# First piece of w1 on ScalarE's DMA queue, two chunk pairs of the weights loaded ahead of x, and the head's products and conversions reordered

## The chip, the cores and the metric

The kernel runs on one core of a Trainium2 chip. The metric is device time in microseconds (us); a run's time is a little longer than its span, which goes from the first to the last instruction of the profiled execution. A measurement of this kernel can tell some 0.2% (0.56 us) from no change.

## The reference, cut to what matters

```python
# x: (4, 512, 512), all in float32; w1, w2: (512, 512)
attn = einsum('ds,td->st', w1, w2) * sparse_mask            # "the mask product"
x = x + gelu(einsum('bds,st->bdt', layernorm(x), attn) + b2) # stage 1
x = x + clustered_ffn(layernorm(x))                          # stage 2
x = x + attention(layernorm(x))                              # stage 3
x = x + clustered_ffn(layernorm(x))                          # stage 4
```

Only the part that has to come before everything else, here called the head, is touched: loading w1 and w2, their product, and the normalized first batch of x that stage 1 multiplies with that product.

## The kernel before, in words

Every engine works through a list written out by hand (`PE_ORDER`, `ACT_ORDER`, `DVE_ORDER`, `POOL_ORDER`, `SP_ORDER`), strictly in order; a step whose input isn't ready holds up all behind it. A step is named kind.key. The steps of the head:

- `load.*` (SyncE, SP): DMA issues. w1 and w2 come in four row chunks each (`load.w1.c`, `load.w2.c`), the first batch of x in four token tiles (`load.x0.t`), the mask in four chunks (`load.sparse.c`), the stage 2 weight in four (`load.ffn.c`); each is 256 KB. `load.cen` is 128 KB.
- Each float32 operand is split in a high and a low part, so that a product is three matmuls (hi*hi, lo*hi, hi*lo). `w1hi.c` (line L558) and `w2hi.c` (L554) on ScalarE (ACT) round a chunk, `w1lo.c` (L743) and `w2lo.c` (L738) on VectorE (DVE) take the remainder.
- `attn.0.0`, `.1`, `.2` (PE, L1019): four matmuls each of chunk 0 into four PSUM banks: hi*hi, w1hi with w2lo, w1lo with w2hi. `attn.1` (PE, L966): all 12 of chunk 1. `last.0` to `last.3`: the 24 of chunks 2 and 3, bank by bank.
- One token tile t of batch 0: `stats.1.0.t` (DVE, L768 and L769), `rstd.1.0.t` (POOL, three dependent instructions: L457, the power at L458, L461), `norm.1.0.t` (ACT, L581), `T.x1.0.t` (PE, four transposes, L1059), then `hi.x1`, `lo.x1`.
- `mask_attn.t` (DVE, L749) multiplies bank t with the mask. `rawhi`, `rawlo` split the result for batch 0, and `y1.0.t.c` are its products.
- POOL sums the four ffn chunks (`fsum.1` to `.3`, L486), then the four chunks of the masked product (`asum.1`, L476, `cmean`, `asum.2`, `asum.3`). `shi` (ACT, L617) and `slo` (DVE, L778) split that sum, and `colmean` (PE, L1079, L1080) forms the column means from it; behind it in PE's list come `y1.0.0.c3` and all else.
- Before that PE runs `WARM` matmuls on a constant (L957), from when POOL's first constant is written.

A wait for a load is on that load's own semaphore:

```python
dve.wait_ge(*landed("x0", t))      # stats.1.0.t
act.wait_ge(*done_at("rstd", key)) # norm.1.0.t
pe.wait_ge(*done_at("norm", (int(what[1]), b, t)))   # T.x1.0.t
pool.wait_ge(*landed("ffn", 0)); pool.wait_ge(*landed("ffn", k))  # fsum.k, k = 1 shown
```

Of the kernel before, what the change touches and what calls it, by code (L numbers as in the profile page):

```python
# [12 lines left out]
P = 128  # L13
# [9 lines left out]
SCALE = float(DH) ** -0.5  # L23
T_BANKS = 4
M_BANKS = 4
WARM = 10

SQUARED = {2, 3, 4}

# [1 line left out]


PE_ORDER = """
attn.0.0 T.x1.0.0 attn.0.1 attn.0.2 T.x1.0.1 attn.1 T.x1.0.2 last.0 last.1 last.2 last.3 T.x1.0.3 y1.0.0.c0
y1.0.2.c0 y1.0.0.c2 T.cen.0.0 y1.0.2.c2 y1.0.3.c02 y1.0.0.c1 colmean y1.0.0.c3 y1.0.1.c3 ffnmean y1.0.2.c1
y1.0.1.c2 y1.0.2.c3 y1.0.1.c10 y1.0.3.c31 y1.1.0.c02 T.x2.0.2 y1.1.0.c3 y1.1.2.c0213 y1.1.0.c1 T.x2.0.0
y1.1.1.c231 y1.1.3.c132 y1.1.1.c0 T.x2.0.3 T.x2.0.1 dn2.0.2.c01 y1.1.3.c0 dn2.0.0.c10 T.x2.1.0 dn2.0.0.c2
# [22 lines left out]
"""  # L60

ACT_ORDER = """
w1hi.0 w2hi.0 norm.1.0.0 w1hi.1 norm.1.0.1 w2hi.1 w2hi.2 w1hi.2 w1hi.3 w2hi.3 norm.1.0.2 hi.x1.0.0 hi.x1.0.2
hi.x1.0.1 rawhi.0 norm.1.0.3 rawhi.2 hi.x1.0.3 ccen rawhi.1 fshi rawhi.3 shi xhi.1.0 ahi.0 gelu.0.0 ahi.2 ahi.3
gelu.0.2 ahi.1 hi.cen.0.0 xhi.1.2 sq.2.0.2 gelu.0.3 xhi.1.3 xhi.1.1 hi.x2.0.2 gelu.0.1 fhi.2 fhi.1 sq.2.0.0
hi.x2.0.0 fhi.0 sq.2.0.3 gelu.1.0 sq.2.0.1 gelu.1.2 fhi.3 hi.x2.0.3 gelu.1.1 hi.x2.0.1 sq.2.1.2 gelu.1.3 xhi.2.0
# [59 lines left out]
"""  # L126

SP_ORDER = """
load.x0.0 load.w1.0 load.w2.0 load.x0.1 load.x0.2 load.w1.1 load.x0.3 load.w2.1 load.w2.2 load.w1.2 load.w1.3
load.w2.3 load.ffn.1 load.ffn.0 load.cen load.ffn.2 load.sparse.0 load.ffn.3 load.sparse.1 load.sparse.2  # L130
load.sparse.3 load.small load.x.1 load.b2 load.xt.1 load.x.3 load.late load.x.2 load.bias load.xt.2 load.xt.3
store.2.3 store.1.0 store.0.0 store.0.1 store.1.3 store.3.2 store.1.1 store.0.3 store.2.1 store.3.0 store.0.2
store.1.2 store.2.0 store.3.1 store.2.2 storeh.3.3.0 storeh.3.3.1
"""

def steps_of(text):

    out = []
    for word in text.split():
        kind, *key = word.split(".")  # L140
        out.append((kind, tuple(int(k) if k.isdigit() else k for k in key)))
    return out
# [55 lines left out]
def program(nc, x_d, xt_d, w1_d, w2t_d, b2_d, sparse_d, wqkv_d, bqkv_d, wo_d, bo_d, ffn_d, fb_d, cen_d,  # L198
            assign_d, out_d):
    ctx = ExitStack()  # L200
    with ctx:
        def sb(name, shape, dt=F32):
            return ctx.enter_context(nc.sbuf_tensor(name, shape, dt))

        def sem(name):
            return ctx.enter_context(nc.semaphore(name))

        x_tok = sb("x_tok", [P, NT, D])
# [9 lines left out]
        w2_raw = sb("w2_raw", [P, KC, D])  # L218
        w1_raw = y_tok[:, KC:2 * KC, :]
# [327 lines left out]

        @block.scalar
        def _(act):
            for kind, key in ACT_STEPS:  # L550
                if kind == "w2hi":
                    c, = key
                    act.wait_ge(*landed("w2", c))
                    act.activation(w2t_hi[:, c, :], w2_raw[:, c, :], ACT.Copy).then_inc(done[kind], 1)  # L554
                elif kind == "w1hi":
                    c, = key
# [26 lines left out]
                elif kind == "hi":  # L583
                    what, b, t = key
# [36 lines left out]
                elif kind == "fhi":  # L621
                    c, = key
# [563 lines left out]
```

## Time and profile before

| what | us |
|---|---|
| median of three runs (lowest, highest) | 278.68 (278.42, 278.83) |
| the profiled execution, its own time | 278.25 |
| its span | 276.5 |
| TensorE matmul busy in it | 268.4 |

A group of rows of the timeline reads: start, duration, engine, line, operation, output<-input, how many, and in brackets the idle time of that engine ahead of it with what ended it. A row "x2" joins two instructions, and its duration reaches from the start of the first to the end of the last. Neighbours on one engine overlap a little in these records.

### The profile page before, as it was taken

What the parts mean: (1) busy time and instruction counts of PE and PEld (TensorE: products, weight loads), DVE (VectorE), ACT (ScalarE), POOL (GpSimd) and SP (SyncE); (2) the same over time, 40 slices, a digit from 0 to 9 for tenths busy, and PEclk for the clock granted to TensorE, in tenths of its full rate; (3) what the DMA queues carried; (4) which work ended last, traced back from release to release, by engine and by line L of the source; (5) the groups of instructions that cost most, each with busy time, mean ns of one, the idle gap of its engine ahead of it and who ended that gap; (6) DMA issues with size and microseconds to landing.
All of it is one profiled execution on the core that took longest, in us unless ns stands there. A gap on an engine that the chain in (4) does not pass through costs nothing.

```text
span 276.5 us, 4419 instructions
## 1 busy us (share of the span) xinstructions
PE 268.4 (97%) x1392; PEld 224.2 (81%) x1392; DVE 196.7 (71%) x410; ACT 176.8 (64%) x358; POOL 158.8 (57%) x192
## 2 busy tenths in 40 slices
PE   7899999999999999999999999999999999999894
PEld 7787888888888888789988888888888888877673
DVE  3888988505926867775399796788259466867996
ACT  4855886465476785449899887777645576675400
POOL 4693988265495481289897994970730537113910
PEclk9999999999999999999999999999999999999998
DMA  6999064800000000000000000000000000000087
GB/s 230 356 370 344 12 207 177 303 0 0 2 0 0 2 0 2 2 0 0 2 0 0 4 1 0 2 0 0 2 2 0 0 2 1 0 2 0 13 306 288
DMA packets 10246, 18.23 MB, mean 66 GB/s; under 512 B 1200, under 2 KB 1968, under 8 KB 10224
## 3 DMA queue, kind: packets, MB, share of 16 engines
q1 hardware_dynamic: 10224, 17.96, 18.5%
q8 instruction: 11, 0.18, 0.3%
q14 instruction: 11, 0.09, 0.1%
HBM read 13.76 MB, written 4.19 MB: 65 GB/s over the span
## 4 chain that ended last, share of the span: by engine, by line
PE 88%; issue 4%; POOL 2%; DVE 2%; DMA 2%; ACT 1%; SPq 1%; DVEq 0%; POOLq 0%; ACTq 0%
PE m_bank L966 70%; PE t_bank L1059 11%; PE m_bank L1139 5%; DMA x_tok<-in_L_attn_a_x 2%; POOL y_tok L546 1%; PE t_bank L1065 1%; PE m_bank L1019 1%; DVE y_tok L925 1%; DVE x_tok L949 0%; ACT odd_hi L613 0%; POOL rstd L458 0%; SPq L384 0%; DVE y_tok L936 0%; SPq L387 0%; PE m_bank L1086 0%
## 5 line engine op out<-in xcount | busy, mean ns | idle before, releaser
L966 PE MATMUL m_bank<-ffn_hi,even_hi 128*128 128x512 f32 x96 | 39.0, 406 | 0.2 <-DVE y_tok L925 0.2
L966 PE MATMUL m_bank<-ffn_lo,even_hi 128*128 128x512 f32 x96 | 37.7, 392 | 0.0
L966 PE MATMUL m_bank<-ffn_hi,even_lo 128*128 128x512 f32 x96 | 37.4, 390 | 0.0
L546 POOL TENSOR_TENSOR y_tok<-y_tok,x_tok 128x512 f32<-128x512 f32 x16 | 20.4, 1296 | 25.4 <-ACT y_tok L719 25.4
L570 ACT ACTIVATE ones_and_squares<-x_tok,mv 128x512 bf16<-128x512 f32 x44 | 31.5, 717 | 4.1 <-DVE x_tok L872 3.7
L526 POOL TENSOR_TENSOR y_tok<-y_tok,bias_f 128x512 f32<-128x512 f32 x16 | 20.8, 1314 | 16.2 <-ACT y_tok L664 16.2
L454 POOL TENSOR_SCALAR ve<-mv 128x1 f32<-128x1 f32 (+1 forms) x20 | 5.3, 264 | 36.1 <-ACT ones_and_squares L570 35.0
L458 POOL TENSOR_TENSOR rstd<-ve,half 128x1 f32<-128x1 f32 (+1 forms) x31 | 23.9, 771 | 2.6
L775 DVE TENSOR_TENSOR even_lo<-t_bank,even_hi 128x512 fp32r<-128x512 f32 x24 | 16.2, 683 | 12.7 <-ACT even_hi L613 12.5
L775 DVE TENSOR_TENSOR odd_lo<-t_bank,odd_hi 128x512 fp32r<-128x512 f32 x28 | 18.8, 685 | 6.2 <-ACT odd_hi L613 6.0
L966 PE MATMUL m_bank<-odd_hi,wqkv_hi 128*128 128x512 f32 (+1 forms) x60 | 21.5, 358 | 0.0
L966 PEld LDWEIGHTS m_bank<-ffn_lo,even_hi 128*128 128x128 f32 x96 | 18.0, 188 | 3.9
L540 POOL TENSOR_TENSOR x_tok<-x_tok,bo 128x512 f32<-128x512 f32 x16 | 21.0, 1331 | 0.0
L966 PEld LDWEIGHTS m_bank<-ffn_hi,even_hi 128*128 128x128 f32 x96 | 18.1, 188 | 3.6 <-DVE y_tok L925 0.6
L966 PE MATMUL m_bank<-odd_lo,wqkv_hi 128*128 128x512 f32 (+1 forms) x60 | 20.9, 348 | 0.0
L966 PE MATMUL m_bank<-odd_hi,wqkv_lo 128*128 128x512 f32 (+1 forms) x60 | 20.8, 347 | 0.0
L966 PEld LDWEIGHTS m_bank<-ffn_hi,even_lo 128*128 128x128 f32 x96 | 18.1, 189 | 3.1
L966 PE MATMUL m_bank<-attn_hi,odd_hi 128*128 128x512 f32 x48 | 19.5, 405 | 0.0
L581 ACT ACTIVATE xn_odd<-x_tok,ve,rstd 128x512 f32<-128x512 f32 x20 | 16.1, 811 | 4.8 <-POOL ve L461 4.8
L966 PE MATMUL m_bank<-attn_lo,odd_hi 128*128 128x512 f32 x48 | 18.8, 391 | 0.0
L966 PE MATMUL m_bank<-attn_hi,odd_lo 128*128 128x512 f32 x48 | 18.7, 390 | 0.0
L613 ACT ACTIVATE even_hi<-t_bank 128x512 fp32r<-128x512 f32 x24 | 13.8, 595 | 6.8 <-PE t_bank L1059 6.8
(186 smaller groups left out, 775.2 us busy)
## 6 DMA issues: line engine op xcount, KB each, us to landing
out<-x_tok SPq DMA_DIRECT2D x15, 256.0 KB, 2.3
x_tok<-in_L_attn_a_x SPq DMA_DIRECT2D x3, 1024.0 KB, 8.2
xn_odd<-in_L_attn_a_xt SPq DMA_DIRECT2D x2, 1024.0 KB, 6.5
x_tok<-in_L_attn_a_x SPq DMA_DIRECT2D x4, 256.0 KB, 4.2
y_tok<-in_L_attn_a_w SPq DMA_DIRECT2D x4, 256.0 KB, 5.1
w_raw<-in_L_attn_a_w SPq DMA_DIRECT2D x4, 256.0 KB, 5.3
xt_other<-in_L_ffn_weight SPq DMA_DIRECT2D x4, 256.0 KB, 6.8
y_tok<-in_L_attn_a_sparse_mask SPq DMA_DIRECT2D x4, 256.0 KB, 7.3
```

Of the source, the lines that this page charges most:

```text
L454: link(pool.tensor_scalar(ve[:, i:i + k], mv[:, i:i + k, 1], 1.0 / D ** 3, EPS, ALU.mult, ALU.add))
L458: ins = pool.tensor_tensor(rstd[:, i:i + k], ve[:, i:i + k], half[:, 0:k], ALU.pow)
L526: pool.tensor_tensor(y_tok[:, n, :], y_tok[:, n, :], bias_f[:, :], ALU.add).then_inc(done[kind], 1)
L540: pool.tensor_tensor(x_tok[:, n, :], x_tok[:, n, :], bo[:, :], ALU.add).then_inc(done[kind], 1)
L546: pool.tensor_tensor(y_tok[:, n, :], y_tok[:, n, :], x_tok[:, n, :], ALU.add).then_inc(done[kind], 1)
L570: act.activation(squares, x_tok[:, n, :], ACT.Square, bias=sum_of(*key), scale=-float(D), accum_out=mv[:, i, 1:2]).then_inc(done[kind], 1)
L581: act.activation(xn_odd[:, t, :], x_tok[:, n, :], ACT.Identity, bias=nbias[:, i:i + 1], scale=rstd[:, i:i + 1]).then_inc(done[kind], 1)
L613: act.activation(split_of(what, b, t)[0], bank_view(what, bank_of("T", *key)), ACT.Copy).then_inc(done[kind], 1)
L775: dve.tensor_tensor(lo, bank_view(what, bank_of("T", *key)), f32(hi), ALU.subtract).then_inc(done[kind], 1)
L966: ins = pe.matmul(bank, a, w, start=(first and n == 0), stop=(last and n == count - 1))
L1059: ins = pe.transpose(bank[:, c * r:(c + 1) * r], blk, ident[0:r, 0:r])
L1139: ins = pe.matmul(bank[:, tokens], cen_hl[:, c, :], a[:, c, tokens], start=(c + h == 0), stop=(c == KC - 1 and h == 1))
```

## The change: what it does, and the diff

ScalarE issues one load of its own, `load.w1.0`, as its very first step. On SyncE's queue the order becomes w2.0, w1.1, w2.1, x0.0, x0.1 and so on: both first chunk pairs of the weights stand ahead of x, and the mask's chunks are mixed in ahead of most of the ffn's. ScalarE converts the first five pieces of the weights before its first norm; VectorE splits two chunk pairs before its first statistics. PE does all products of chunks 0 and 1 before its first transpose, and has 11 warm-up matmuls in place of 10. Nothing else in any list moves.

```diff
-WARM = 10
+WARM = 11
...
 PE_ORDER = """
-attn.0.0 T.x1.0.0 attn.0.1 attn.0.2 T.x1.0.1 attn.1 T.x1.0.2 last.0 last.1 last.2 last.3 T.x1.0.3 y1.0.0.c0
+attn.0.0 attn.0.2 attn.0.1 attn.1 T.x1.0.0 T.x1.0.1 T.x1.0.2 last.0 last.1 last.2 last.3 T.x1.0.3 y1.0.0.c0
...
 ACT_ORDER = """
-w1hi.0 w2hi.0 norm.1.0.0 w1hi.1 norm.1.0.1 w2hi.1 w2hi.2 w1hi.2 w1hi.3 w2hi.3 norm.1.0.2 hi.x1.0.0 hi.x1.0.2
+w1hi.0 w2hi.0 w1hi.1 w2hi.1 w2hi.2 norm.1.0.0 w1hi.2 norm.1.0.1 w1hi.3 w2hi.3 norm.1.0.2 hi.x1.0.0 hi.x1.0.2
...
 DVE_ORDER = """
-stats.1.0.0 w1lo.0 stats.1.0.1 stats.1.0.2 w2lo.0 stats.1.0.3 w1lo.1 w2lo.1 w2lo.2 w1lo.2 w1lo.3 w2lo.3
+w1lo.0 w2lo.0 w1lo.1 w2lo.1 stats.1.0.0 stats.1.0.1 w2lo.2 w1lo.2 stats.1.0.2 w1lo.3 w2lo.3 stats.1.0.3
...
 SP_ORDER = """
-load.x0.0 load.w1.0 load.w2.0 load.x0.1 load.x0.2 load.w1.1 load.x0.3 load.w2.1 load.w2.2 load.w1.2 load.w1.3
-load.w2.3 load.ffn.1 load.ffn.0 load.cen load.ffn.2 load.sparse.0 load.ffn.3 load.sparse.1 load.sparse.2
-load.sparse.3 load.small load.x.1 load.b2 load.xt.1 load.x.3 load.late load.x.2 load.bias load.xt.2 load.xt.3
+load.w2.0 load.w1.1 load.w2.1 load.x0.0 load.x0.1 load.w2.2 load.w1.2 load.x0.2 load.w1.3 load.w2.3 load.x0.3
+load.sparse.0 load.sparse.1 load.cen load.sparse.2 load.ffn.1 load.sparse.3 load.ffn.0 load.ffn.2 load.ffn.3
+load.small load.x.1 load.b2 load.xt.1 load.x.3 load.late load.x.2 load.bias load.xt.2 load.xt.3 store.2.3
...
+AQ_ORDER = "load.w1.0"
+AQ_STEPS = steps_of(AQ_ORDER)
...
         @block.scalar
         def _(act):
+            for _, (what, c) in AQ_STEPS:
+                if what == "w1":
+                    act.dma_start(w1_raw[:, c, :], w1_d[c * P:(c + 1) * P, :]).then_inc(ld[what, c], 16)
```

## Rows read from the trace of the kernel before

**Rows 1.** The page: busy time by engine, and the chain that ended last.

```profile
PE 268.4 (97%) x1392; PEld 224.2 (81%) x1392; DVE 196.7 (71%) x410; ACT 176.8 (64%) x358; POOL 158.8 (57%) x192
...
PE 88%; issue 4%; POOL 2%; DVE 2%; DMA 2%; ACT 1%; SPq 1%; DVEq 0%; POOLq 0%; ACTq 0%
```

**Rows 2.** One long stretch of PE: stretch, length, busy, granted clock, DMA.

```profile
19.95:245.00 225.05, 224.97 (x1184) 1.00 0.10 34
```

**Rows 3.** Timeline of PE, 0 to 15 us.

```profile
0.98 4.44 PE L957 MATMUL m_bank<-ones_and_squares 128*128 128x128 f32 x20 [0.98 <-POOL ones_and_squares L433]
6.25 1.16 PE L1019 MATMUL m_bank<-w2t_hi,even_hi 128*128 128x512 f32 x4 [0.84 <-issue]
...
14.07 0.47 PE L966 MATMUL m_bank<-w2t_hi,even_hi 128*128 128x512 f32 x1
```

**Rows 4.** The chain that ended last, in order of time (start, length).

```profile
14.31 5.48 PE m_bank L966 x24
```

**Rows 5.** Timeline of ScalarE, 0 to 15 us.

```profile
0.72 1.28 ACT L558 ACT_TABLE_LOAD   x1 [0.72 <-PEq L1174]
3.95 0.63 ACT L558 ACTIVATE even_hi<-y_tok 128x512 fp32r<-128x512 f32 x1 [1.95 <-DMA y_tok<-in_L_attn_a_w]
5.53 0.63 ACT L554 ACTIVATE w2t_hi<-w_raw 128x512 fp32r<-128x512 f32 x1 [0.94 <-DMA w_raw<-in_L_attn_a_w]
...
8.66 0.82 ACT L581 ACTIVATE xn_odd<-x_tok,ve,rstd 128x512 f32<-128x512 f32 x1 [0.39 <-POOL ve L461]
9.38 1.14 ACT L554 ACTIVATE w2t_hi<-w_raw 128x512 fp32r<-128x512 f32 x2
```

**Rows 6.** Timeline of VectorE, 0 to 15 us.

```profile
6.20 0.69 DVE L768 BATCH_NORM_STATS2 st<-x_tok 128x6 f32<-128x512 f32 x1 [0.89 <-DMA x_tok<-in_L_attn_a_x]
...
7.03 0.68 DVE L768 BATCH_NORM_STATS2 st<-x_tok 128x6 f32<-128x512 f32 x1
...
10.03 1.29 DVE L738 TENSOR_TENSOR w2t_lo<-w_raw,w2t_hi 128x512 fp32r<-128x512 f32 x2
```

**Rows 7.** Timeline of POOL, 0 to 24 us.

```profile
7.19 0.23 POOL L457 TENSOR_SCALAR ve<-mv 128x1 f32<-128x1 f32 x1 [1.08 <-DVE mv L769]
...
10.11 0.70 POOL L457 TENSOR_SCALAR ve<-mv 128x1 f32<-128x1 f32 x1
...
11.86 0.79 POOL L461 TENSOR_SCALAR ve<-mv,rstd 128x1 f32<-128x1 f32 x1
13.96 1.29 POOL L486 TENSOR_TENSOR y_tok<-xt_other 128x512 f32<-128x512 f32 x1 [1.31 <-DMA xt_other<-in_L_ffn_weight]
...
19.99 3.21 POOL L476 TENSOR_TENSOR y_tok<-y_tok 128x512 f32<-128x512 f32 x2
```

**Rows 8.** DMA issues of 9.7 to 10.2 us: the issue, and its time to landing.

```profile
9.76 0.43 SPq L390 DMA_DIRECT2D y_tok<-in_L_attn_a_sparse_mask  x1
y_tok<-in_L_attn_a_sparse_mask SPq DMA_DIRECT2D x1, 256.0 KB, 7.2
```

**Rows 9.** Stretches of the DMA: length, granted clock, DMA share, GB/s.

```profile
3.50:4.00 0.50, 1.00 0.70 164
...
5.00:6.00 1.00, 1.00 1.03 381
```

**Rows 10.** Timeline, 23 to 26 us: `shi`, `slo`, `colmean`.

```profile
23.23 0.63 ACT L617 ACTIVATE wo_hi<-y_tok 128x512 fp32r<-128x512 f32 x1 [0.20 <-POOL y_tok L476]
...
23.89 0.69 DVE L778 TENSOR_TENSOR wo_lo<-y_tok,wo_hi 128x512 fp32r<-128x512 f32 x1
...
25.48 0.40 PE L1079 MATMUL t_bank<-wo_hi,mean_of 128*128 128x512 f32 x1
```

**Rows 11.** Stretches behind the last matmul: PE, PEld, DVE, ACT, POOL busy, PEclk, DMA.

```profile
272.50:273.00 0.50, 0.13 (x2) 0.00 (x0) 0.50 (x1) 0.00 (x0) 0.00 (x0) 1.00 1.03 389
...
274.50:275.00 0.50, 0.00 (x0) 0.00 (x0) 0.00 (x0) 0.00 (x0) 0.00 (x0) 0.73 0.90 316
275.00:275.50 0.50, 0.00 (x0) 0.00 (x0) 0.00 (x0) 0.00 (x0) 0.00 (x0) 0.50 0.83 279
```

More of the change, by code:

```diff
@@ L128 @@
 SP_ORDER = """
-load.x0.0 load.w1.0 load.w2.0 load.x0.1 load.x0.2 load.w1.1 load.x0.3 load.w2.1 load.w2.2 load.w1.2 load.w1.3
-load.w2.3 load.ffn.1 load.ffn.0 load.cen load.ffn.2 load.sparse.0 load.ffn.3 load.sparse.1 load.sparse.2
-load.sparse.3 load.small load.x.1 load.b2 load.xt.1 load.x.3 load.late load.x.2 load.bias load.xt.2 load.xt.3
-store.2.3 store.1.0 store.0.0 store.0.1 store.1.3 store.3.2 store.1.1 store.0.3 store.2.1 store.3.0 store.0.2
-store.1.2 store.2.0 store.3.1 store.2.2 storeh.3.3.0 storeh.3.3.1
+load.w2.0 load.w1.1 load.w2.1 load.x0.0 load.x0.1 load.w2.2 load.w1.2 load.x0.2 load.w1.3 load.w2.3 load.x0.3
+load.sparse.0 load.sparse.1 load.cen load.sparse.2 load.ffn.1 load.sparse.3 load.ffn.0 load.ffn.2 load.ffn.3
+load.small load.x.1 load.b2 load.xt.1 load.x.3 load.late load.x.2 load.bias load.xt.2 load.xt.3 store.2.3
+store.1.0 store.0.0 store.0.1 store.1.3 store.3.2 store.1.1 store.0.3 store.2.1 store.3.0 store.0.2 store.1.2
+store.2.0 store.3.1 store.2.2 storeh.3.3.0 storeh.3.3.1
 """
+AQ_ORDER = "load.w1.0"
 def steps_of(text):
@@ L294, in program @@
         m_bank = [ctx.enter_context(nc.psum_tensor(f"m_bank{i}", [P, 512], F32)) for i in range(M_BANKS)]
-        ld = {key: sem("ld_" + "_".join(str(k) for k in key)) for kind, key in SP_STEPS if kind == "load"}
+        ld = {key: sem("ld_" + "_".join(str(k) for k in key)) for kind, key in SP_STEPS + AQ_STEPS if kind == "load"}
         done = {kind: sem(kind + "_done") for kind in COUNT}
@@ L549, in _ @@
         def _(act):
+            for _, (what, c) in AQ_STEPS:
+                if what == "w1":
+                    act.dma_start(w1_raw[:, c, :], w1_d[c * P:(c + 1) * P, :]).then_inc(ld[what, c], 16)
+                elif what == "w2":
+                    act.dma_start(w2_raw[:, c, :], w2t_d[c * P:(c + 1) * P, :]).then_inc(ld[what, c], 16)
+                else:
+                    act.dma_start(x_tok[:, c, :], x_d[0][c * P:(c + 1) * P, :]).then_inc(ld[what, c], 16)
             for kind, key in ACT_STEPS:
```

## The prediction

> **What bounds the kernel now.** I read the page first: PE is busy for 268.4 of 276.5 us, and 88% of the chain that ended last is its own [rows 1]. Then one long stretch of PE: from 19.95 us, where the first `y1` starts, to 245 us it is busy for 224.97 of 225.05 us [rows 2]. So there is nothing behind the head that could take up a delay or a gain: what the head moves, the end moves by as much, as long as the other engines keep up with a shifted PE. Last I read the head engine by engine. PE finishes its 10 warm-ups at 0.98 + 4.44 = 5.42 us, begins `attn.0.0` at 6.25 us and `last.0` at 14.07 us [rows 3]. A matmul costs 5.48/24 = 0.228 us [rows 4]. Of the 7.8 us between those two starts, 24 matmuls take 5.5 us and three groups of transposes some 0.57 us each, 1.7; only 0.6 us is idle. The start of `attn.0.0` is set by w2.0, third in the queue, whose conversion ran from 5.53 to 6.16 us [rows 5]. Loads come one behind the other, so I read a landing from the engine that waited for it: second in the queue 3.95, third 5.53 [rows 5], fourth 6.20 [rows 6], fourteenth (`ffn.0`) 13.96 [rows 7], and after 18.5 pieces of 256 KB (`sparse.1`) 9.76 + 7.2 = 16.96 us [rows 8].
>
> **The change, first sum: when does `last.0` start?** The weights come earlier, but the three norms now stand behind them, and each `rstd` is a trip over VectorE, POOL and ScalarE.
>
> Prices. Conversion: 0.63 us, the next starts 1.14 - 0.63 = 0.51 us later [rows 5]. Remainder: 0.69, the next 1.29 - 0.69 = 0.60 us later [rows 6]. Statistics: 7.03 - 6.20 = 0.83 us from one to the next [rows 6], and 7.19 - 6.20 = 0.99 us to POOL's first instruction [rows 6, 7]. From there to the norm: 8.66 - 7.19 = 1.47 us [rows 5, 7]; the trip beside VectorE's conversions took 11.86 + 0.79 - 10.11 = 2.54 us [rows 7]. I take 1.5 for each and keep 2.54 as the upper bound. A norm is 0.82 us [rows 5], and I let the next step start 0.70 us after it.
>
> I give each load the landing of its place. w1.0 (ScalarE's queue) and w2.0 share places one and two: 3.95 us. w1.1 is third, 5.53; w2.1 fourth, 6.20. ScalarE: `w1hi.0` 3.95, `w2hi.0` 4.46, `w1hi.1` 5.53, `w2hi.1` 6.20 to 6.83. VectorE: `w2lo.1` 6.87, so `stats.1.0.0` starts at 7.47 (x0.0, fifth, is there at about 6.95). POOL begins at 8.46, `norm.1.0.0` at 9.96. **Behind that norm `w1hi.2` is queued**, though its data are long there: 10.66. Behind it wait `w1lo.2` (11.32) and, in VectorE's list, `stats.1.0.2` (11.92), although x0.2 is there. POOL 12.91, `norm.1.0.2` 14.4, its end 15.2, `T.x1.0.2` to 15.85. The two trips that overlapped with the loads before now stand one behind the other.
>
> PE meanwhile: the eleventh warm-up costs 0.44 us and ends at 5.86 us (without it `attn.0.0` could start at 5.1, but nothing is won by that, since PE waits later anyway). 24 matmuls from 5.86 end at 11.3; `T.x1.0.0` is ready (norm ended 10.8); `norm.1.0.1` needs the second POOL trip, 11.4 to 12.2, so `T.x1.0.1` ends at 12.8, and PE stands idle until 15.3. `last.0` starts at 15.9 where it was 14.07: **1.8 us later**. In parts: start of `attn.0.0` 0.4 earlier, idle time 2.2 longer. `w2lo.3` isn't what is late: about 14.0 by the same steps.
>
> Bounds. ScalarE's DMA issue isn't in this trace. Its nearest row is SyncE's, 0.43 us [rows 8], and the table load at 0.72 us, done at 2.0 [rows 5]; if the issue stands behind that load, w1.0 lands near 4.7 us, and `stats.1.0.0` moves by only 0.3 us, since w2.1 set it. At the other end a second queue could fill the dip that the DMA has at 3.5 to 4.0 us, 164 GB/s against 381 a little later [rows 9]: at most 0.7 us earlier for all that follows. Then `last.0` is late by 1.1 us; and with the weights there at once, VectorE's own chain (`w1lo.0` at 3.3 + 0.63, four remainders of 0.60, then as above) still leaves 0.8. Two slow trips make it 1.8 + 2 x 1.04 = 3.9 us.
>
> The Trainium skill (DMA: Bandwidth & Descriptors, section Issuing engines are not separate DMA queues) says that transfers issued from several engines run on the same 16 DMA engines and that only the issuing time is saved. The trace agrees as far as it goes: the DMA is full from 5 us on with one queue issuing [rows 9]. By that rule the two first loads share a place each as above, the dip isn't filled, and the sum stays at 1.8.
>
> **Second sum: `colmean`.** `ffn.0`, fourteenth before, now has 18.5 pieces up to its end: 16.96 us in place of 13.96. POOL's `fsum.1` waits for it, and all three `fsum` stand ahead of `asum` in POOL's list; from `fsum.1` to the end of `asum.3` POOL is busy but for hand-offs (13.96 to 19.99 + 3.21 = 23.20 us) [rows 7]. `ffn.2` and `ffn.3` follow at (16.96 - 13.96)/4.5 = 0.67 us each, faster than POOL's 1.29 us. So `asum.3` ends 3.0 us later, at 26.2; `shi` and `slo`, which followed at once [rows 10], end at 26.9 and 27.6. PE's `colmean` stood at 25.48 us, 0.9 us after `slo` [rows 10]. With the first sum alone it would come at 27.3; now it waits until 27.65: **2.2 us later than before**, whatever the first sum is between 0 and 2.2. `rawlo.3`, one place behind `slo` on VectorE, ends at 28.2, and `y1.0.0.c3`, due two matmuls after `colmean`, waits 0.1 us more. Masks come earlier in the queue, and PE never waited for them: nothing.
>
> The sum: 2.3 us. The profiled execution would take 278.25 + 2.3 = 280.55, and the median, 0.43 above it, **281.0 us**. Taking slower trips into account the likeliest case reaches from 280.3 to 281.8.
>
> **The rivals.**
>
> - *The clock falls too.* PE is idle from 12.8 to 15.3 us, with nothing but transposes from 11.3. Behind its last matmul (over by 272.63 us) the granted clock was still 1.00 until 274.5 and then fell, within that stretch, to 0.50, which is 1.2 GHz [rows 11]: after about 2.1 us of idleness. For: the new gap is 2.5 us. Against: before, at 5.4 and 7.9 us, only gaps under 1 us occurred, so no row shows a fall within work. Price: the 24 matmuls of `last` at twice 0.228 us cost 5.5 us at most; the warm-ups ran 4.44 us, and as long at half speed loses 2.2 us. Of that 0.5 is hidden behind POOL's chain: +4.0, **282.7 us**. The Trainium skill (TensorE: Matmul & The Clock Gate, Part 4: PE-mode transpose) adds that transposes don't count as the same kind of PE activity; by it this rival has more for it, since the quiet stretch would begin at 11.3 us. No row here parts the two.
> - *The second queue fills the dip.* All loads 0.7 us earlier: `last.0` +1.1, `colmean` +1.6 because POOL's chain moves with `ffn.0`: **280.3 us**.
> - *Faster: PE is fed throughout.* Then the 0.4 us of the earlier start and the 0.6 idle are both won, 1.0 us: **277.7 us**. Its place is `norm.1.0.2`: it would have to start by 12.6 us rather than 14.4 (14.07 less 0.57 of transposes, 0.82 of norm and the hand-off), and `ffn.0` would have to land by 14.9. For it speaks only that the transfers before 5 us are slow; the dip gives 0.7 of those 1.8 us.
> - *Nothing to be seen.* With loads or trips 1.8 us shorter `last.0` starts where it did, but POOL's chain is still late by 3.0 - 1.8 = 1.2 us, less the 0.9 of slack at `colmean`: 0.3 us, **279.0 us**.
>
> **How the numbers follow.** Likeliest case 0.53, clock 0.17, dip filled 0.13, fed 0.09, nothing 0.08. The time is that of the first, 281.0. The range takes in the first three, 279.7 to 283.2; below it lie the last two, 0.17. Faster by over 0.2%: 0.09; within: 0.09 (with the low edge of the dip's case); slower: 0.82.
>
> **What the profile of the changed kernel would show.** `attn.0.0` at 5.9 us right behind the warm-ups; `norm.1.0.0` near 10 us with `w1hi.2` right behind it; PE idle before `T.x1.0.2`, with the norm as releaser, `last.0` near 15.9; POOL's `fsum.1` released by the ffn load near 17 us; `colmean` near 27.7 us, waiting for VectorE; no idle time of PE after that, so that the rest runs as before. Wrong would be: `last.0` at or before 14.1 with `colmean` at or before 25.5; loads that land well ahead of their places; a granted clock of 0.50 behind the gap, which would put the end another 1.7 us later.

## The result and the profile after

The changed kernel takes **281.95 us** (median of four runs, 281.76 to 283.12) against 278.55 us in the four runs of the kernel before (278.38 to 278.83): a ratio of 1.0125, 95% interval 1.0103 to 1.0147, so 3.4 us slower. Predicted were 281.0 us, from 279.7 to 283.2. The profiled execution took 281.8 us, its span is 279.9 us. The time lies near the one predicted, but POOL's hold on `colmean`, one of the two sums that lead there, did not happen, and what took its place, a fall of the clock, is a rival that the prediction held unlikely. All lines below are of the changed kernel until the experiments; its code stands 12 lines further down (the norm, L581 before, is L593).

The page, the rows that answer to [rows 1]:

```profile
PE 270.3 (97%) x1394; PEld 225.8 (81%) x1394; DVE 196.7 (70%) x410; ACT 176.5 (63%) x358; POOL 157.6 (56%) x192
...
PE 86%; issue 4%; POOL 3%; DVE 3%; ACT 2%; DMA 1%; DVEq 0%; POOLq 0%; ACTq 0%
```

PE is busy for 1.9 us more than before though it has only two instructions more (the eleventh warm-up). So the lost time isn't all idleness: some of PE's work took longer. The stretches of PE (from:to, length, busy, granted clock, DMA share, GB/s) say where:

```profile
14.00:15.00 1.00, 0.00 (x0) 1.00 1.06 389
15.00:16.00 1.00, 0.51 (x5) 0.92 1.05 385
16.00:17.00 1.00, 1.00 (x5) 0.50 1.15 335
17.00:18.00 1.00, 1.00 (x4) 0.50 1.05 332
18.00:19.00 1.00, 1.00 (x4) 0.50 1.02 371
19.00:20.00 1.00, 1.00 (x5) 0.87 1.07 397
...
23.44:245.00 221.56, 221.48 (x1163) 1.00 0.09 32
```

The last row answers to [rows 2]: from the first `y1` on PE is busy without a break, as before, and everything is decided ahead of 23.44 us. Rows two to six are new: as PE sets to work again after a pause the granted clock is 0.50, which is 1.2 GHz: three full rows and parts of two, 2 x 0.08 + 3 + 2 x 0.13 = 3.4 us. PE's timeline:

```profile
0.98 4.91 PE L969 MATMUL m_bank<-ones_and_squares 128*128 128x128 f32 x22 [0.98 <-POOL ones_and_squares L437]
5.64 1.17 PE L1031 MATMUL m_bank<-w2t_hi,even_hi 128*128 128x512 f32 x4
...
11.21 1.40 PE L1071 MATMUL t_bank<-ident,xn_odd 128*128 128x128 f32 x8
15.49 0.83 PE L1071 MATMUL t_bank<-ident,xn_odd 128*128 128x128 f32 x4 [2.89 <-ACT xn_odd L593]
15.97 0.78 PE L978 MATMUL m_bank<-w2t_hi,even_hi 128*128 128x512 f32 x1
16.55 0.63 PE L978 MATMUL m_bank<-w2t_hi,even_lo 128*128 128x512 f32 x1
16.97 0.63 PE L978 MATMUL m_bank<-w2t_lo,even_hi 128*128 128x512 f32 x1
...
19.41 0.39 PE L978 MATMUL m_bank<-w2t_lo,even_hi 128*128 128x512 f32 x1
...
23.44 0.48 PE L978 MATMUL m_bank<-even_hi,odd_hi 128*128 128x512 f32 x1
...
28.93 0.40 PE L1091 MATMUL t_bank<-wo_hi,mean_of 128*128 128x512 f32 x1
```

The whole loss stands in it in two parts. `last.0` starts at 15.97 us where it was 14.07 [rows 3]: **1.90 us**, and the pause ahead of it, 2.89 us, has the norm of tile 2 as its releaser. The first `y1` of the kernel before started at 19.98 us (the 19.95 in the prediction is the start of the stretch of [rows 2], in which the transposes ahead of it end):

```profile
19.98 0.48 PE L966 MATMUL m_bank<-even_hi,odd_hi 128*128 128x512 f32 x1
```

From `last.0` to the first `y1` it is 7.47 us, where it was 19.98 - 14.07 = 5.91: **1.56 us** for the same 24 matmuls, which come at first every 0.43 us (16.97 - 16.55 = 0.42) instead of 0.23; the eight steps from 15.97 to 19.41 took 3.44 us, against 8 x 0.228 = 1.8. Together 3.46 us, the shift of `y1` and, within 0.1, of the span. Nothing is added later: `colmean` comes 28.93 - 23.44 = 5.49 us after the first `y1`, as before (25.48 - 19.98 = 5.50) [rows 10].

What the norm of tile 2 waited for is read on ScalarE, then VectorE, then POOL.

```profile
0.72 0.41 ACTq L556 DMA_DIRECT2D y_tok<-in_L_attn_a_w  x1
1.15 1.28 ACT L570 ACT_TABLE_LOAD   x1 [1.15 <-PEq L1186]
4.14 0.63 ACT L570 ACTIVATE even_hi<-y_tok 128x512 fp32r<-128x512 f32 x1 [1.71 <-DMA y_tok<-in_L_attn_a_w]
...
9.74 0.82 ACT L593 ACTIVATE xn_odd<-x_tok,ve,rstd 128x512 f32<-128x512 f32 x1 [1.35 <-POOL ve L465]
10.46 0.61 ACT L570 ACTIVATE even_hi<-y_tok 128x512 fp32r<-128x512 f32 x1
...
14.63 0.81 ACT L593 ACTIVATE xn_odd<-x_tok,ve,rstd 128x512 f32<-128x512 f32 x1 [1.70 <-POOL ve L465]
```

```profile
7.30 0.69 DVE L780 BATCH_NORM_STATS2 st<-x_tok 128x6 f32<-128x512 f32 x1
...
11.11 0.69 DVE L755 TENSOR_TENSOR even_lo<-y_tok,even_hi 128x512 fp32r<-128x512 f32 x1 [1.54 <-ACT even_hi L570]
11.72 0.69 DVE L780 BATCH_NORM_STATS2 st<-x_tok 128x6 f32<-128x512 f32 x1
...
27.37 0.69 DVE L790 TENSOR_TENSOR wo_lo<-y_tok,wo_hi 128x512 fp32r<-128x512 f32 x1 [0.15 <-ACT wo_hi L629]
```

```profile
12.71 0.57 POOL L461 TENSOR_SCALAR ve<-mv 128x1 f32<-128x1 f32 x1 [1.66 <-DVE mv L781]
...
16.10 1.28 POOL L490 TENSOR_TENSOR y_tok<-xt_other 128x512 f32<-128x512 f32 x1 [0.15 <-DMA xt_other<-in_L_ffn_weight]
...
21.38 1.29 POOL L480 TENSOR_TENSOR y_tok<-y_tok 128x512 f32<-128x512 f32 x1 [1.28 <-DVE y_tok L761]
```

ScalarE idles for 1.35 us ahead of `norm.1.0.0`, with `w1hi.2` queued right behind it (10.46); VectorE idles 1.54 us for that (11.11), with `stats.1.0.2` queued behind; POOL idles 1.66 us for that (12.71); ScalarE again 1.70 us (14.63). That is one convoy: a row of waits that one late step hands on through three ordered lists. One stretch of the DMA (the columns before the last three are PE, PEld, DVE, ACT, POOL) was a dip of 164 GB/s before [rows 9]:

```profile
3.50:4.00 0.50, 0.50 (x4) 0.50 (x4) 0.00 (x0) 0.00 (x0) 0.00 (x0) 1.00 1.05 393
```

### The profile page after: what moved, and what is told of

Same layout as the page of the kernel before. It is cut to its first block, busy times and chain, and to the rows that moved or that the text cites. A ratio compares the mean times of both kernels' runs of the same rounds, so it can differ in the third digit from the quotient of the medians.

```text
span 279.9 us, 4423 instructions
## 1 busy us (share of the span) xinstructions
PE 270.3 (97%) x1394; PEld 225.8 (81%) x1394; DVE 196.7 (70%) x410; ACT 176.5 (63%) x358; POOL 157.6 (56%) x192
## 4 chain that ended last, share of the span: by engine, by line
PE 86%; issue 4%; POOL 3%; DVE 3%; ACT 2%; DMA 1%; DVEq 0%; POOLq 0%; ACTq 0%
PE m_bank L978 69%; PE t_bank L1071 11%; PE m_bank L1151 5%; POOL y_tok L550 1%; DMA y_tok<-in_L_attn_a_w 1%; PE t_bank L1077 1%; POOL rstd L462 1%; DVE y_tok L937 1%; ACT xn_odd L593 1%; DVE even_lo L755 0%; DVE st L780 0%; DVE w2t_lo L750 0%; ACT even_hi L570 0%; DVE x_tok L961 0%; ACT odd_hi L625 0%
## 5 line engine op out<-in xcount | busy, mean ns | idle before, releaser
L593 ACT ACTIVATE xn_odd<-x_tok,ve,rstd 128x512 f32<-128x512 f32 x20 | 16.1, 812 | 7.5 <-POOL ve L465 7.5
```

The source lines that it names most:

```text
L593: act.activation(xn_odd[:, t, :], x_tok[:, n, :], ACT.Identity, bias=nbias[:, i:i + 1], scale=rstd[:, i:i + 1]).then_inc(done[kind], 1)
```

## The experiments

Each ratio is to the kernel before, run beside it on the same chip, with its 95% interval. The questions: is the pause really made by `w1hi.2` behind the norm; what do the clock, the loads and POOL's chain each cost; and is anything in the change worth keeping.

**e1: the pause filled with matmuls on a constant.**

```diff
-... T.x1.0.0 T.x1.0.1 T.x1.0.2 last.0 ...
+... T.x1.0.0 T.x1.0.1 fill.0 T.x1.0.2 last.0 ...
+                elif kind == "fill":
+                    for _ in range(11):
+                        pe.matmul(t_bank[T_BANKS - 1][:, 0:P], mean_raw[:, :], mean_raw[:, :], start=True, stop=True)
```

> The changed kernel with 11 more matmuls on a constant between T.x1.0.1 and T.x1.0.2 (their results are overwritten), which fill PE's idle stretch from 12.6 to 15.4 us; the wait for the norm stays. If the fall of the granted clock is a cost of its own, the clock stays at 1.00, last.0 still starts near 16.0 us, the 24 matmuls of last take 5.5 us rather than 7.0, and the kernel takes some 280.5 us, 1.5 less than the changed kernel's 281.95. If the reduced pace is hidden behind POOL's chain, as the second sum of the prediction has it, less than 0.5 us comes back. If the clock has nothing to do with the idle stretch it falls again and nothing changes.

Measured: 281.11 us (280.76 to 282.61), ratio 1.0094 (1.0072 to 1.0116). The filling ran from 12.68 to 15.30 us, the clock stayed at 1.00 (0.997 to 0.999 as mean of each of the six runs, where the changed kernel had 0.987 to 0.993), and `last.0` started at 16.15 us. The fall is gone, but only 0.84 us with it, where some 1.5 were expected. In the profile `last.0` came 0.18 us later, and a new wait for `rawlo.0` on VectorE took 0.67 back ahead of `y1.0.0` (22.73 - 16.15 = 6.58 us from `last.0` to it in place of 5.91; 0.42 of it shows as idle, and I put the rest down to lost overlap): 1.56 - 0.18 - 0.67 = 0.71 us. That instruction took 1.37 us in place of 0.68 while POOL added two SBUF tiles beside it, and returned to 0.68 behind it:

```profile
21.22 1.37 DVE L766 TENSOR_TENSOR even_lo<-y_tok,even_hi 128x512 fp32r<-128x512 f32 x1
22.51 0.68 DVE L766 TENSOR_TENSOR wqkv_lo<-y_tok,wqkv_hi 128x512 fp32r<-128x512 f32 x1
```

```profile
20.74 1.30 POOL L480 TENSOR_TENSOR y_tok<-y_tok 128x512 f32<-128x512 f32 x1
```

**e2: `w1hi.2` ahead of `norm.1.0.0`**, nothing else, to take out the link of the convoy that the prediction named.

```diff
-w1hi.0 w2hi.0 w1hi.1 w2hi.1 w2hi.2 norm.1.0.0 w1hi.2 norm.1.0.1 w1hi.3 ...
+w1hi.0 w2hi.0 w1hi.1 w2hi.1 w2hi.2 w1hi.2 norm.1.0.0 norm.1.0.1 w1hi.3 ...
```

> The changed kernel with one swap: w1hi.2 ahead of norm.1.0.0 on ScalarE. If the two trips standing one behind the other are what makes last.0 late, stats.1.0.2 starts near 10.1 rather than 11.7 us, norm.1.0.2 near 12.9 rather than 14.6, last.0 near 14.3 rather than 16.0, and the clock stays up since the gap is about 1 us. What is left then is POOL's chain: fsum.1 still near 16.1, 2.1 us later than before, so that colmean comes at about 26.75 rather than 25.7 and the kernel takes some 279.8 us. If POOL's chain doesn't bind, 278.8. If the norms aren't the cause, it stays near 282.

Measured: 280.59 us (280.28 to 281.69), 1.0077 (1.0057 to 1.0097), 0.8 us above the expected 279.8. `stats.1.0.2` started at 10.19 us in place of 11.72, `last.0` at 14.72, PE's pause ahead of `T.x1.0.2` shrank to 1.09 us. The link is shown. But the same shape had moved one place on: `stats.1.0.3` now stood behind `w1lo.3` and `w2lo.3`, `rstd.1.0.3` behind it, and POOL's whole chain behind that:

```profile
15.26 0.22 POOL L461 TENSOR_SCALAR ve<-mv 128x1 f32<-128x1 f32 x1 [2.28 <-DVE mv L781]
```

Its first addition, `fsum.1`, started at 16.61 us, and the later ones thus came beside `rawlo.0` and the next remainder again (1.41 and 1.77 us), and `y1.0.0` waited 0.47 us. Three of the six runs had a mean clock of 1.0 and took 280.28 to 280.41 us; the other three (0.990 to 0.992) took 280.78 to 281.69. That the clock would stay up behind a pause of 1 us was expected wrongly.

**e3: only the queue**, the kernel before with w1.0 issued by ScalarE.

```diff
-load.x0.0 load.w1.0 load.w2.0 load.x0.1 ...
+load.x0.0 load.w2.0 load.x0.1 ...
+AQ_ORDER = "load.w1.0"
```

> The kernel before, in which only load.w1.0 moves to ScalarE's queue; all lists else as before. If the second queue fills the dip of the DMA between 3.5 and 4.5 us, w2.0 lands about 1 us earlier, attn.0.0 starts near 5.5 rather than 6.25 us, loads up to w2.1 land 0.6 us earlier, and the kernel takes about 278.0 us, 0.5 less than before. If only issue time is saved, it takes 278.55 as before.

Measured: 278.03 us (12 runs, 277.76 to 279.06), 0.9977 (0.9956 to 0.9998), as expected. The dip is gone, and `last.0` starts at 13.81 us, 0.26 earlier:

```profile
3.50:4.00 0.50, 0.50 (x4) 0.50 (x4) 0.00 (x0) 0.00 (x0) 0.00 (x0) 1.00 1.02 381
```

PE starts the products at 5.53 us, 0.7 earlier, but gives most of it back at once: it now waits 0.90 us for the first norm ahead of `T.x1.0.0`. The start of the products is not the second queue's doing alone: w2.0, which they wait for, is now second on SyncE's queue and was third.

**e4: e2 with the ffn's loads ahead of the mask's**, as in the kernel before: does the late `ffn.0` hold POOL's chain?

```diff
-load.sparse.0 load.sparse.1 load.cen load.sparse.2 load.ffn.1 load.sparse.3 load.ffn.0 load.ffn.2 load.ffn.3
+load.ffn.1 load.ffn.0 load.cen load.ffn.2 load.sparse.0 load.ffn.3 load.sparse.1 load.sparse.2 load.sparse.3
```

> As the run with w1hi.2 first, and the ffn chunks loaded ahead of the mask's again, as in the kernel before. If POOL's chain, started by ffn.0, bound there, fsum.1 now starts near 13.5 us, colmean comes at about 25.7, and the kernel takes some 278.8 us, 1.0 less than that run. If it didn't bind, the two runs take the same.

Measured: 280.41 us (280.09 to 280.74), 1.0062 (1.0046 to 1.0077): the expected 278.8 is missed, and the time is that of e2. `fsum.1` started at 16.39 us with no wait for a transfer; what stood ahead of it in POOL's list was `rstd.1.0.3`, at 15.19 us, 2.28 us of idleness ahead of it. The order of the mask and ffn loads is worth nothing that can be seen as long as that is so: the runs of e2 without a fall took 280.28 to 280.41 us. And in e4 the clock did not fall in any of the six runs (0.999 to 1.0), though PE's pause ahead of `T.x1.0.2` was 1.09 us as in e2. POOL's chain did reach PE here. `colmean` started 0.15 us behind the end of `slo`, 27.11 - 21.13 = 5.98 us after `y1.0.0`, where it is 5.50 in the kernel before:

```profile
26.27 0.69 DVE L790 TENSOR_TENSOR wo_lo<-y_tok,wo_hi 128x512 fp32r<-128x512 f32 x1
```

```profile
27.11 0.47 PE L1091 MATMUL t_bank<-wo_hi,mean_of 128*128 128x512 f32 x1
```

**e5: e4 with `stats.1.0.3` ahead of the last two remainders**, the link that e2 and e4 showed.

```diff
-... w2lo.2 w1lo.2 stats.1.0.2 w1lo.3 w2lo.3 stats.1.0.3
+... w2lo.2 w1lo.2 stats.1.0.2 stats.1.0.3 w1lo.3 w2lo.3
```

> As the run with w1hi.2 first and the ffn chunks early, and stats.1.0.3 moved ahead of w1lo.3 and w2lo.3 on VectorE. In that run fsum.1 started at 16.4 us although its data were there: it stands behind rstd.1.0.3 in POOL's list, whose statistics came at 14.2 us. If this is what starts POOL's chain late, fsum.1 now starts near 14.4 us, colmean comes at PE's own slot near 26.1 rather than 27.1, rawlo.0 is back at 0.7 us, and the kernel takes some 279.4 us, 1.0 less. If POOL's chain never bound, it stays at 280.4.

Measured: 279.56 us (279.38 to 280.64), 1.0048 (1.0031 to 1.0065), within 0.2 us of the expected 279.4. `fsum.1` starts at 15.15 us, `last.0` at 14.76, `y1.0.0` at 21.15. Up to `y1.0.0` nothing is won over e4 (21.13); from there to `colmean` it is 26.63 - 21.15 = 5.48 us in place of 5.98. Those 0.5 us of the span's 0.8 (278.4 to 277.6) are what POOL's late chain had cost: in e4 its additions stretched the remainder of `rawlo.2` to 1.77 us (0.68 here), and `colmean` came right behind `slo`.

**e6: `T.x1.0.2` behind `last.1`**, so that PE need not wait for the norm.

```diff
-... T.x1.0.1 T.x1.0.2 last.0 last.1 last.2 last.3 ...
+... T.x1.0.1 last.0 last.1 T.x1.0.2 last.2 last.3 ...
```

> The changed kernel with one step of PE's list moved: T.x1.0.2 behind last.1 instead of ahead of last.0. PE then waits only for w2lo.3, done at 13.8 us in the changed kernel, so last.0 starts near 13.9 rather than 16.0 us, PE's gap is 1.3 us and the granted clock stays at 1.00. If PE's start of last were all, the kernel would take 278.4 us; with POOL's chain as it is (fsum.1 at 16.1 us) colmean can't come before 26.8 us, and I expect 279.9 us. If the weights rather than the third norm are late, it stays near 282.

Measured: 283.07 us (280.66 to 283.85), 1.0154 (1.0121 to 1.0186): a miss, slower than the changed kernel, though `last.0` starts at 13.79 us, 0.3 us earlier than before the change. The clock fell all the same, and here it fell twice:

```profile
13.00:14.00 1.00, 0.21 (x1) 1.00 1.07 377
14.00:15.00 1.00, 1.00 (x3) 0.53 1.06 387
...
24.00:25.00 1.00, 1.00 (x4) 0.65 0.48 49
25.00:26.00 1.00, 1.00 (x4) 0.50 0.71 190
```

```profile
13.79 0.58 PE L978 MATMUL m_bank<-w2t_hi,even_hi 128*128 128x512 f32 x1 [1.25 <-DVE w2t_lo L750]
...
22.70 0.66 PE L1071 MATMUL t_bank<-ident,xn_odd 128*128 128x128 f32 x4 [1.10 <-ACT xn_odd L593]
```

`last.0` is released by `w2lo.3`, so the norm of tile 2 is what the changed kernel had waited for. Pauses of 1.25 us, and later of 1.10 and 0.56 us, stood ahead of the two falls. The runs order themselves by the clock: 280.66 us at a mean of 0.998, 282.26 and 282.43 at 0.992 and 0.994, 283.70 to 283.85 at 0.985 and 0.986. The expected 279.9 was a sum without the clock; the one run without a fall came to 280.66.

**e7: an order meant to feed PE throughout**, x and the weights mixed, with ten warm-ups.

```diff
-load.w2.0 load.w1.1 load.w2.1 load.x0.0 load.x0.1 load.w2.2 load.w1.2 load.x0.2 load.w1.3 load.w2.3 load.x0.3
+load.w2.0 load.x0.0 load.x0.1 load.w1.1 load.w2.1 load.x0.2 load.w2.2 load.w1.2 load.x0.3 load.w1.3 load.w2.3
...
-w1hi.0 w2hi.0 w1hi.1 w2hi.1 w2hi.2 norm.1.0.0 w1hi.2 norm.1.0.1 w1hi.3 w2hi.3 norm.1.0.2
+w1hi.0 w2hi.0 w1hi.1 norm.1.0.0 w2hi.1 w2hi.2 norm.1.0.1 w1hi.2 w1hi.3 norm.1.0.2 w2hi.3
...
-w1lo.0 w2lo.0 w1lo.1 w2lo.1 stats.1.0.0 stats.1.0.1 w2lo.2 w1lo.2 stats.1.0.2 w1lo.3 w2lo.3 stats.1.0.3
+w1lo.0 stats.1.0.0 w2lo.0 stats.1.0.1 w1lo.1 w2lo.1 stats.1.0.2 w2lo.2 w1lo.2 stats.1.0.3 w1lo.3 w2lo.3
```

(The ffn's loads ahead of the mask's as in e4; on PE `T.x1.0.0` ahead of `attn.1`.)

> A version meant to beat both: w1.0 on ScalarE's queue, then w2.0, x0.0, x0.1, w1.1, w2.1, x0.2, w2.2, w1.2, x0.3, w1.3, w2.3, with the statistics spread so that each POOL trip runs beside conversions, and PE doing attn.0.0, attn.0.2, attn.0.1, T.x1.0.0, attn.1, T.x1.0.1, T.x1.0.2, last. If PE is fed, last.0 starts near 13.0 us, 1.1 before the kernel before, and it takes about 277.4 us. If only the landing of w2.3 counts, it takes about 278.0 as with the queue alone; if a trip stands in a queue again, more.

Measured: 279.97 us (279.84 to 280.07), 1.0052 (1.0040 to 1.0064): a miss by 2.6 us, by the mechanism of the change itself, which I had put back in at two places. `w2hi.1` stood behind `norm.1.0.0`, `w2hi.3` behind `norm.1.0.2`, and ScalarE ran each right behind its norm, with no wait for a load. `last.0` started at 15.62 us, where 13.0 was expected:

```profile
8.61 0.81 ACT L588 ACTIVATE xn_odd<-x_tok,ve,rstd 128x512 f32<-128x512 f32 x1 [1.32 <-POOL ve L465]
9.33 1.13 ACT L561 ACTIVATE w2t_hi<-w_raw 128x512 fp32r<-128x512 f32 x2
...
13.50 0.82 ACT L588 ACTIVATE xn_odd<-x_tok,ve,rstd 128x512 f32<-128x512 f32 x1 [1.29 <-POOL ve L465]
14.22 0.61 ACT L561 ACTIVATE w2t_hi<-w_raw 128x512 fp32r<-128x512 f32 x1
```

**e8: e3 with `attn.0.2` ahead of `T.x1.0.0`**, to fill the 0.90 us that e3 showed.

```diff
-attn.0.0 T.x1.0.0 attn.0.1 attn.0.2 T.x1.0.1 attn.1 ...
+attn.0.0 attn.0.2 T.x1.0.0 attn.0.1 T.x1.0.1 attn.1 ...
```

> The kernel before with w1.0 on ScalarE's queue, and attn.0.2 ahead of T.x1.0.0 and attn.0.1 in PE's list (the one part of the change's PE order for which the data are there). It fills the 0.9 us that PE waited for the first norm. But attn.1 then waits for w2lo.1, done at 10.45 us, where it started at 10.6: so only 0.15 us is won, 277.9 us against 278.0 with the queue alone. If PE's idle time in front of the first transpose is worth its full length, 277.1.

Measured: 278.21 us (12 runs, 277.76 to 278.68), 0.9983 (0.9972 to 0.9994). The early wait is gone, another stands later: 0.57 us ahead of `attn.1` for `w2lo.1`. `last.0` starts at 13.74 us against 13.81 in e3. No gain over e3 is shown.

**e9: e8 with the second pair earlier**: w2.1 loaded ahead of x0.3, `w2hi.1` ahead of `norm.1.0.1`, `w1lo.1` and `w2lo.1` ahead of `stats.1.0.3`.

```diff
-... load.w1.1 load.x0.3 load.w2.1 ...      # SP
+... load.w1.1 load.w2.1 load.x0.3 ...
-... w1hi.1 norm.1.0.1 w2hi.1 w2hi.2 ...    # ACT
+... w1hi.1 w2hi.1 norm.1.0.1 w2hi.2 ...
-... w2lo.0 stats.1.0.3 w1lo.1 w2lo.1 ...   # DVE
+... w2lo.0 w1lo.1 w2lo.1 stats.1.0.3 ...
```

> As the run with attn.0.2 moved, and the second chunk pair a step earlier: w2.1 loaded ahead of x0.3, w2hi.1 ahead of norm.1.0.1 on ScalarE, w1lo.1 and w2lo.1 ahead of stats.1.0.3 on VectorE. No conversion then stands behind a norm whose trip isn't over. w2lo.1 should end near 9.5 us, attn.1 start near 10.0 and last.0 near 13.3 rather than 13.8: 277.4 us. If a conversion behind a norm costs nothing there, 277.9 as with PE's swap alone.

Measured: **277.79 us** (12 runs, 277.40 to 279.35), 0.9973 (0.9959 to 0.9987): faster than the kernel before, with the lowest median of all versions, though 0.4 us above the expected 277.4; against e3 and e8 the intervals overlap. PE has no pause over 0.2 us from 5.69 to 30 us:

```profile
9.48 0.66 PE L1066 MATMUL t_bank<-ident,xn_odd 128*128 128x128 f32 x4 [0.17 <-ACT xn_odd L588]
...
13.22 0.47 PE L973 MATMUL m_bank<-w2t_hi,even_hi 128*128 128x512 f32 x1
```

`last.0` is 0.85 us earlier than in the kernel before [rows 3], the span 0.7 us shorter.

**e10: e5 with w1.0 first on SyncE's queue**, none on ScalarE's: the second queue's worth in the changed order.

```diff
-load.w2.0 load.w1.1 load.w2.1 ...
+load.w1.0 load.w2.0 load.w1.1 load.w2.1 ...
-AQ_ORDER = "load.w1.0"
+AQ_ORDER = ""
```

> As the run with the statistics of tile 3 early (279.56 us), but w1.0 issued first on SyncE's queue and none on ScalarE's. If the second queue is what fills the DMA's dip at 3.5 to 4.5 us, the dip is back, w2.0 lands near 4.1 us as the second in the queue but w2.1 near 6.2, stats.1.0.0 starts 0.1 us or so later, later loads 0.5 us later, and the kernel takes 279.7 to 280.1 us. If the queue alone is worth 0.6 us here as in the kernel before, 280.2. If it makes nothing here, 279.6.

Measured: 280.43 us (279.68 to 280.78), 1.0060 (1.0042 to 1.0078), 0.87 us more than e5 by the medians, on another chip. Part of that is the clock: the runs with a mean of 1.0 are 279.68, 279.93 and 280.29 us here, and those at 0.998 and above 279.38 to 279.62 in e5, so some 0.45 us remain at an equal clock; the others, at 0.991 and 0.992, are 280.57 to 280.78 here and 280.49 and 280.64 there. In the profiles `last.0` starts at 14.96 us against 14.76. A slow start of the DMA isn't back. There are slower half microseconds (201 GB/s from 2.5 to 3.0 us, 274 from 4.5 to 5.0), but e5 has such ones too (188 from 2.0 to 2.5, 262 from 5.0 to 5.5), and over the first 5.5 us e10, with one queue, moved as much as e5 (261 GB/s from 1.0 to 5.5 us) and the changed kernel (267). The kernel before, then e10:

```profile
1.00:5.50 4.50, 4.42 (x20) 4.22 (x20) 1.57 (x3) 1.63 (x2) 2.43 (x10) 1.00 0.72 235
```

```profile
1.00:5.50 4.50, 4.50 (x21) 4.50 (x22) 1.52 (x3) 2.89 (x4) 1.50 (x8) 1.00 0.82 267
```

**e11: e1 with transposes for the filling**, to part two causes of the fall: an idle PE, or a PE that does nothing but transposes.

```diff
-                    for _ in range(11):
-                        pe.matmul(t_bank[T_BANKS - 1][:, 0:P], mean_raw[:, :], mean_raw[:, :], start=True, stop=True)
+                    for _ in range(22):
+                        pe.transpose(t_bank[T_BANKS - 1][:, 0:P], ident[:, :], ident[:, :])
```

> The changed kernel with 22 dummy transposes of the identity between T.x1.0.1 and T.x1.0.2, where e1 had 11 dummy matmuls; by 0.57 to 0.70 us for four of them (T.x1) they cover 2.6 to 3.3 us of the gap of 2.89 us. Theory A (transposes don't hold the clock, it falls because nothing but transposes and idleness stand between 11.2 and 15.5 us): the granted clock falls to 0.50 as it did without the filling, near 15.5 to 16 us or a little earlier, the products of last run at 0.43 us apiece for some 3.3 us, y1.0.0 starts near 23.4 to 23.6 us, the mean granted clock of most runs is 0.987 to 0.993, and the median is that of the changed kernel, 281.7 to 282.3. Theory B (only an idle PE lets it fall, a transpose counts as work): the clock stays at 1.00 in nearly all runs, y1.0.0 near 22.7 us and the median 281.1 as in e1. A fall that comes before 15 us, while the transposes run, would be the clearest sign for A.

Measured: 280.99 us (7 runs, 280.47 to 281.97), 1.0080 (1.0050 to 1.0109), the mean clock 0.997 to 1.0 in every run. From 11.82 to 15.25 us PE did only transposes, four more at 15.51, and the products behind them ran at full pace:

```profile
12.69 2.56 PE L1040 MATMUL t_bank<-ident 128*128 128x128 f32 x22
15.51 0.65 PE L1074 MATMUL t_bank<-ident,xn_odd 128*128 128x128 f32 x4 [0.26 <-ACT xn_odd L593]
15.92 0.47 PE L978 MATMUL m_bank<-w2t_hi,even_hi 128*128 128x512 f32 x1
```

Here transposes held the clock as well as matmuls did: the pause itself let it fall, theory A is out. `y1.0.0` started at 22.21 us, 1.23 before the changed kernel, with `last.0` only 0.05 earlier. Most of the 1.56 us is thus won back in this profile, while e1 lost half of it again to `rawlo.0`.

## Why the prediction was right, and where it was not

**First sum (when `last.0` starts): right.** Predicted 1.8 us later, measured 1.90, and nearly every station with it: `w1hi.2` 10.66 against 10.46, `stats.1.0.2` 11.92 against 11.72, `norm.1.0.2` 14.4 against 14.63, `last.0` 15.9 against 15.97. e2 shows the cause by taking it away: one swap on ScalarE brings `last.0` forward by 1.25 us of the 1.90. `stats.1.0.0` started at 7.30 us where I had 7.47, and for another reason: I let w2.1 set it, but the loads of the second pair came 0.3 to 0.5 us ahead of my steps (`w1hi.1` 5.20, `w2hi.1` 5.72), and VectorE's own four remainders, back to back from 4.88 us, set it. The third trip took back as much and more: 14.63 - 11.72 = 2.91 us from `stats` to norm, where I had 0.99 + 1.5. The upper bound that I kept, 2.54 us for POOL's part, wasn't reached (14.63 - 12.71 = 1.92). The eleventh warm-up can have cost nothing, since the pause of 2.89 us takes it up; no run leaves it out.

**Loads by place: wrong, on the safe side.** I gave each load the landing of its place, the second queue's too. But `ffn.0`, to land at 16.96 us, let `fsum.1` start at 16.10, 0.86 us ahead of its place (0.2 in e1, with the same loads on another chip: 16.73). ScalarE's issue took 0.41 us and stood ahead of its table load, so the bound of a w1.0 that comes behind that load fell away. The dip at 3.5 us was filled, 393 GB/s where 164 had been. e3 does that alone in the kernel before (381 GB/s, `last.0` 0.26 us earlier, ratio 0.9977, its interval only just clear of 1). The Trainium skill (DMA: Bandwidth & Descriptors, section Issuing engines are not separate DMA queues) says that only issuing time is saved; in e3 the dip was filled, which that sentence had not led me to expect. But e10 fills it too, with one queue and another order of the loads (267 GB/s from 1.0 to 5.5 us against 235), so the second queue isn't shown to be the cause; the order of the loads, or the one execution that was profiled of each kernel, may be. I had the filled dip as a rival at 0.13. Its loads came early in part, by 0.3 to 0.5 us in place of 0.7, but its effect on `last.0` (1.1 in place of 1.8) did not come: w1.0 itself was converted at 4.14 us, not before 3.95, and from there VectorE's list and the convoy set `last.0`.

**Second sum (`colmean` waits for POOL's chain, 2.2 us whatever the first sum is): this step failed.** In the changed kernel it never waited: 5.49 us after the first `y1`, as before, with `slo` over at 27.37 + 0.69 = 28.06 and `colmean` at 28.93. Three things together: the chain began 0.9 us earlier than its place; PE was later than my first sum had it, by the clock; and the chain then waited for PE in its turn (`asum.1` idle 1.28 us for VectorE's product with the mask). Nor did it bind in e1, where the clock held: 28.24 - 22.73 = 5.51 us. Where POOL does reach PE is mostly another way that I had not priced: its additions lengthen VectorE's remainders from 0.68 to between 1.37 and 1.77 us in e1 and e2, just ahead of the first `y1` (0.42 us of idleness of PE in e1, 0.47 in e2). In e2 and e4, where `y1.0.0` came 2.1 and 2.3 us earlier than in the changed kernel, `colmean` did start right behind `slo` (0.15 us after its end); by the spacing of the products, 0.23 us, it lost only some 0.07 us by that. So the 0.5 us that I added for the changed kernel was wrong as a mechanism.

**The clock (a rival, chance 0.17): it happened.** Price 2.2 us foretold, 1.56 measured. I had taken the length of the warm-ups, 4.44 us, for the stretch at half speed; it lasted 3.4 us, and half of that is 1.7. What spoke against it was that no pause of PE over 1 us was to be seen in the profile before; the only row of a fall stood behind 2.1 us of idleness [rows 11], and the new pause was 2.89. That should have had more than 0.17. e1 and e11 show that the pause is the cause: filled, by either kind of work, none of thirteen runs fell, where all four of the changed kernel had. The Trainium skill (TensorE: Matmul & The Clock Gate, Part 4: PE-mode transpose) says that a transpose doesn't count as PE-busy the same way; in e11 it made no difference, and the clock stayed at 1.00 through 3.4 us of transposes alone.

**The sum.** Forecast was 1.8 + 0.5 = 2.3 us; it was 1.90 + 1.56 = 3.5 us in the profile and 3.4 by the medians. The two terms are those of the clock's rival, 1.8 + 2.2 with POOL's chain hidden behind them, the second one oversized by 0.6. The forecast came within 1.0 us because its wrong half microsecond stood in for a third of the missing 1.6; that part of it is luck. Where PE's long pause comes from and how long it is, was right; what a pause costs was not.

**Open.** What makes the clock fall in some runs of e2, e5, e6 and e10 and not in others, with pauses of 1.1 to 1.3 us, and in none of e4 with the same. Two of 63 runs of the kernel before that were taken beside the experiments also had a mean of only 0.991 and 0.993 (281.32 and 279.74 us), though its profile shows no pause over 0.84 us behind the start. And e10's medians against e5's: some 0.45 us at an equal clock, of which the profiles show 0.3 (spans of 277.9 and 277.6); the chips differ. What made the DMA slow from 3.5 to 4.5 us in the profile of the kernel before is open too.

## What to carry to other kernels

In lists that engines work through strictly in order, look at each step that waits for a trip over other engines and ask what stands behind it with its data already there: here one rounding behind one norm cost 1.3 us of start, and a second like it hid right behind. A pause of PE has two prices, its length and the pace of the work behind it; a forecast with a new pause as long as those here (1.1 to 2.9 us) needs both, and a version that feeds PE a little earlier but in bursts can be slower than one that feeds it evenly (e6 against e9). A block moved as a whole is best tried link by link: the queue alone gained 0.6 us by its ratio (0.26 at `last.0` in its profile), with a milder order (e9) 0.75, while the whole reordering cost 3.4.

## What the runs showed of the hardware that I had not expected

- The granted clock fell to 0.50 within work, behind pauses of 2.89 us (all four runs of the changed kernel) and also of 1.1 to 1.3 us (three of six runs of e2 and of e10, two of six of e5, five of six of e6, none of six of e4), and in the profiles of the changed kernel and of e6 it stayed there for 3.4 us each time. In e3, with a pause of 0.90 us, and in e7, e8 and e9, with none over 0.6 us up to `last.0`, none of the 42 runs had a mean under 0.997. One fall costs 0.8 to 1.7 us here: 1.56 by the path of the changed kernel; by the medians of the runs with and without one, 1.1 in e5, 0.9 in e2, 0.8 in e10 and 1.7 in e6.
- The granted clock does not show every change of pace. The 20 instructions of the warm-up took 4.44 us [rows 3], 0.22 us each, and 22 of the same shape in e1, from 12.68 us on, took 2.62 us, 0.12 each; the profiles give a clock of 1.00 for both stretches. Why is not shown.
- 22 transposes of 0.12 us held the clock at 1.00 as 11 float32 matmuls of 0.24 us did.
- VectorE's subtraction with both inputs in SBUF (0.68 us) took 1.37 to 1.77 us in e1 and e2 while POOL added two SBUF tiles (1.30 us; other such remainders took 0.97 us in the kernel before and 1.18 in e5), and POOL's own addition then took up to 1.74 us (e2; 1.73 in e4); with one input in PSUM (the product with the mask) VectorE kept its 0.69. In e1 the stretched one ended 22.59 - 22.04 = 0.55 us behind POOL's addition, and in e2 22.90 - 22.35 = 0.55, as if it had run only then. The Trainium skill (GPSIMD Engine Reference, section Specifications) names a contention of the two engines for VectorE instructions with two SBUF inputs; the traces agree.
- At 3.5 to 4.0 us the DMA moved 164 GB/s in the kernel before, 381 to 393 with one load on ScalarE's queue (e3 and the changed kernel), but also 356 with a single queue and the changed order (e10).
